# A 16-sample attention and graph-convolution kernel: a new order of work on every engine

## The reference

```
x = x + attention(_gn(x))                  # _gn: groups of 2 channels
    q = softmax(q over 32 channels of a head) * scale;  k = softmax(k over 1024 pixels)
    context = k @ v^T;  out = context^T @ q;  out = w_out @ out + b_out
    out = normalised over the whole sample, * gn_weight + gn_bias
x = x + graph_conv(_gn(x))
    xn  = pixels' 64-vectors scaled to length 1;  sim = xn @ xn^T      # 1024 x 1024 per sample
    val, idx = top_k(sim, 9);  v = val / sum(val)
    out = sum over 9 neighbours of v * (xn @ w1) + b1;  group norm (4 groups), silu
    out = sum over the same neighbours of v * (out @ w2) + b2;  group norm, silu
```

## Time and profile before

| | us |
|---|---|
| median of 3 runs | 694.48 (687.77 to 695.98) |
| the profiled execution | 693.69 |
| its span, first to last instruction | 691.9 |
| TensorE busy, share of the span | 623.0, 90% |
| VectorE | 536.2, 77% |
| GpSimd | 499.6, 72% |
| ScalarE | 449.3, 65% |
| DMA queue of SyncE, share of 16 engines | 38.8% |
| granted TensorE clock, mean | 0.978 |

### The profile page before, as it was taken

One profiled execution on the slowest core, in us unless ns is written; L12 is line 12 of the kernel. 1 busy time (PEld: TensorE's weight loads), 2 busy tenths in 40 slices (PEclk: granted clock), 3 DMA queues, 4 the chain that ended last, 5 costly groups with the idle time before them and its releaser, 6 DMA issues.

```text
span 691.9 us, 12330 instructions
## 1 busy us (share of the span) xinstructions
PE 623.0 (90%) x3821; PEld 312.0 (45%) x3821; DVE 536.2 (77%) x1008; ACT 449.3 (65%) x942; POOL 499.6 (72%) x534
## 2 busy tenths in 40 slices
PE   7787979898999999998999999998989999889984
PEld 5563635344353535353444535353534444333441
DVE  2238788888898989888898889898888988857821
ACT  2236658586786878585867768786858687643321
POOL 0122787868787888888797978888887979786810
PEclk9999999999999999999999999999999999979997
DMA  3002343434354444435353535435343634454311
GB/s 93 0 17 46 71 83 78 91 71 107 83 102 84 100 85 93 92 83 102 76 110 77 108 76 107 85 86 103 83 96 71 108 63 101 82 96 88 62 32 31
DMA packets 148722, 55.76 MB, mean 81 GB/s; under 512 B 138008, under 2 KB 138512, under 8 KB 148656
## 3 DMA queue, kind: packets, MB, share of 16 engines
q1 hardware_dynamic: 148656, 54.97, 38.8%
HBM read 12.87 MB, written 4.32 MB: 25 GB/s over the span
## 4 chain that ended last, share of the span: by engine, by line
PE 31%; POOL 25%; issue 16%; DVE 10%; DMA 9%; ACT 7%; SPq 1%; POOLq 0%; ACTq 0%; DVEq 0%
PE pC L967 17%; POOL adj L389 10%; POOL adj L384 5%; PE pS L923 4%; DMA rbc<-rn_row 4%; DMA rn_row<-rnT 4%; POOL qn L348 3%; ACT adj L527 2%; PE pB L768 2%; POOL res L407 2%; DVE kstat L607 2%; ACT ek L458 2%; PE pA L807 2%; POOL xn L372 2%; DVE top L676 2%
## 5 line engine op out<-in xcount | busy, mean ns | idle before, releaser
L967 PE MATMUL pC<-adj,xt 128*64 128x512 f32 x992 | 233.2, 603 | 3.1 <-POOL adj L395 1.8
L389 POOL TENSOR_TENSOR adj<-maskT,adj 128x128 f32<-128x128 f16 (+3 forms) x127 | 163.6, 1288 | 28.2 <-DMA maskT<-mask 25.3
L676 DVE MAX8 top<-pS 128x8 f32<-128x1024 f32 x128 | 155.6, 1224 | 30.7 <-ACT adj L527 30.5
L694 DVE MATCH_REPLACE8 mask<-top,pS 128x1024 uint16<-128x1024 f32 x128 | 155.3, 1213 | 0.0
L923 PE MATMUL pS<-xn 64*128 64x512 f32 x256 | 145.3, 655 | 6.2 <-issue 5.6
L923 PE MATMUL pS<-xn,xsw 64*128 64x512 f32 x256 | 144.7, 656 | 2.9 <-DVE mask L694 2.9
L527 ACT COPY adj<-pS 128x1024 f32<-128x1024 f32 x128 | 128.3, 1004 | 27.3 <-PE pS L925 27.1
L384 POOL TENSOR_TENSOR adj<-maskT,adj 128x128 f32<-128x128 f16 (+6 forms) x111 | 128.5, 1158 | 0.0
L967 PEld LDWEIGHTS pC<-adj,xt 128*64 128x64 f32 x992 | 63.9, 137 | 103.6 <-issue 96.0
L395 POOL TENSOR_TENSOR adj<-adj,selves 128x128 f32<-128x128 f32 x127 | 58.7, 462 | 8.7
L925 PEld LDWEIGHTS pS<-mark,place 64*128 64x128 f16 x256 | 24.5, 96 | 76.1 <-issue 76.1
(11 more groups left out here) (153 smaller groups left out, 1101.7 us busy)
## 6 DMA issues: line engine op xcount, KB each, us to landing
xs<-x SPq DMA_DIRECT2D x32, 128.0 KB, 2.8
vbc<-v_row SPq DMA_DIRECT2D x32, 128.0 KB, 2.9
rbc<-rn_row SPq DMA_DIRECT2D x30, 128.0 KB, 2.8
xsw<-xn SPq DMA_DIRECT2D x30, 128.0 KB, 2.4
out<-res SPq DMA_DIRECT2D x30, 128.0 KB, 2.4
maskT<-mask SPq DMA_TRANSPOSE x128, 3.1
cst<-packed SPq DMA_DIRECT2D x1, 471.5 KB, 3.9
y1sw<-y SPq DMA_DIRECT2D x2, 128.0 KB, 2.3
```

The lines of the kernel that those rows point to most:

```text
L389: pool.tensor_tensor(above, m[:, r, 0:r + 1, :].bitcast(F16), above, ALU.mult).then_inc(done["upper"], 1)
L676: dve.max(top[b % 2][:, r, 0:TOP], pS[r % 2][:, :]).then_inc(done["tile_top"], 1)
L694: dve.match_replace(out=mask[n % MASKS][:, :], in_to_replace=top[b % 2][:, r, 0:TOP], in_values=pS[r % 2][:, :], imm_value=ONE_BITS).then_ ...
L967: mm = pe.matmul(ps[h * C:(h + 1) * C, 0:H], xt[:, t % NJ, t // NJ, :], adj[b % 2][:, t, h * H:(h + 1) * H], start=(t == 0), stop=(t == NT ...
```

## The change

The single list `BEGINS` becomes three, one each for attention and unit, for the tile stages, and for convolve; `PARTS` says which stage takes which list. All the offsets in `TIMES` are replaced, and so is `WARM`: 318 fillers become 390 (a group for `("q", 1)` is in the table, but no step asks for it). In four places waits of TensorE follow the new order, and one call of `warm` is dropped. No instruction that computes is added or removed.

```diff
-BEGINS = [0, 40.3551, 80.6227, 121.0734, 161.3839, 202.0138, 242.3515, 282.6959, 323.22, 363.5685, 404.1094, 444.49,
...
+PARTS = {"inputs": 0, "attend": 0, "unit": 0, "weights": 1, "itself": 1, "neighbours": 1, "tops": 1, "masks": 1, "marks": 1, "convolve": 2}
+BEGINS = [
...
-    ("start", 0): 36, ("k", 0): 20, ("ekT", 0): 9, ("qT", 0): 8, ("att", 0): 7, ("at_mean", 0): 16, ("in_mean", 1): 6,
-    ("mi_mean", 0): 32, ("k", 1): 9, ("ss", 0): 4, ("att", 1): 6, ("sim1", 0): 2, ("mi_mean", 1): 24, ("k", 2): 9,
-    ("xt1", 1): 24, ("g1_mean", 14): 18, ("sim7", 15): 12, ("g2_mean", 14): 18, ("g1_mean", 15): 12, ("xt2", 15): 21,
-    ("a2_0", 15): 5, ("ky", 0): 20,
+    ("start", 0): 36, ("k", 0): 24, ("ekT", 0): 9, ("qT", 0): 8, ("att", 0): 8, ("at_mean", 0): 19, ("in_mean", 1): 10,
+    ("mi_mean", 0): 39, ("k", 1): 17, ("q", 1): 8, ("att", 1): 9, ("in_mean", 2): 10, ("sim4", 0): 16, ("mi_mean", 1): 10,
+    ("k", 2): 13, ("xt1", 1): 18, ("sim0", 1): 16, ("att", 2): 9, ("g1_mean", 14): 2, ("sim7", 15): 13, ("xt2", 14): 7,
+    ("g2_mean", 14): 11, ("g1_mean", 15): 12, ("xt2", 15): 29, ("a2_0", 15): 4, ("g2_mean", 15): 21, ("ky", 0): 20,
...
-                    live += [(BEGINS[b] + at, steps) for at in TIMES[engine][stage.__name__]]
+                    live += [(BEGINS[PARTS[stage.__name__]][b] + at, steps) for at in TIMES[engine][stage.__name__]]
...
                 if b < 1:
                     pe.wait_ge(*of("in_veps", b))
+                elif b < 2:
+                    pe.wait_ge(*of("ss_read", b - 1, 2))
                 else:
                     pe.wait_ge(*of("mi_veps", b - 1))
...
-                warm("ss", b)
                 pe.wait_ge(*of("sq_ready", b))
-                if b < 15:
+                if b < 1:
+                    pe.wait_ge(*of("mi_veps", b))
+                elif b < 15:
                     pe.wait_ge(*of("yT_copied", b + 1))
...
                 pe.wait_ge(*of("rn_ready", b))
-                if b < 2:
+                if b < 1:
+                    pe.wait_ge(*of("yT_copied", b + 1))
+                elif b < 2:
                     pe.wait_ge(*of("ss_read", b, 2))
```

More of the change, by code:

```diff
@@ L29 @@
 PACKED = CONST_PARTS + WEIGHT_PARTS + [(name, 1) for name in VECTORS]
-BEGINS = [0, 40.3551, 80.6227, 121.0734, 161.3839, 202.0138, 242.3515, 282.6959, 323.22, 363.5685, 404.1094, 444.49,
-          485.0099, 525.4191, 565.7534, 605.859]
+PARTS = {"inputs": 0, "attend": 0, "unit": 0, "weights": 1, "itself": 1, "neighbours": 1, "tops": 1, "masks": 1, "marks": 1, "convolve": 2}
+BEGINS = [
+    [0, 43.7679, 84.6436, 125.8457, 167.2382, 207.6013, 248.8792, 289.8169, 330.7721, 372.2689, 413.5082, 454.2157, 495.8963,
+     536.5253, 577.4959, 618.5594],
+    [0, 40.7602, 81.636, 122.8463, 163.4119, 204.6215, 245.3367, 286.5808, 327.994, 369.0126, 409.9847, 451.4971, 492.2687,
+     533.3503, 573.6684, 613.2583],
+    [0, 40.9091, 81.6341, 122.584, 163.4381, 204.3951, 245.6569, 286.9489, 328.1214, 369.3658, 410.7502, 451.3767, 492.5799,
+     532.9203, 574.8846, 614.585],
+]
 TIMES = {
@@ L37 @@
         "attend": [0],
-        "unit": [122.814, 124.0739, 139.8554],
-        "neighbours": [144.5435, 146.5376, 153.5254, 159.4181, 159.4182, 168.0831, 180.5052, 181.0079],
-        "convolve": [199.2326, 199.2327, 265.073],
+        "unit": [89.7538, 96.4524, 103.3671],
+        "neighbours": [120.9276, 121.1054, 133.105, 133.1051, 133.1052, 143.4386, 152.7499, 160.4412],
+        "convolve": [169.202, 170.4109, 233.8618],
     },
     "gpsimd": {
-        "attend": [60.859, 84.8058],
-        "unit": [99.5701, 99.5702, 104.0019, 106.8089, 112.4974],
@@ L45 @@
[L45 to L48, removed]
+        "attend": [58.9225, 84.1612],
+        "unit": [90.8105, 96.6084, 105.8733, 110.5569, 119.5039],
+        "weights": [138.195, 140.4417, 144.0865, 144.0866, 146.2015, 149.0325, 150.4153, 151.0194, 151.0195, 151.0196,
+            155.3908, 157.5535, 157.6905, 157.6906, 158.8454, 168.3563, 168.3564, 168.3565, 171.6202, 171.8558, 171.8559,
+            174.0678, 174.9659],
@@ L49 @@
+        "convolve": [197.0726, 216.224, 247.7607],
     },
     "scalar": {
[L51 to L55, removed]
+        "attend": [54.954, 68.1936, 73.202, 79.3721, 79.4966, 82.3873, 85.7675, 90.3689, 96.448, 99.9077],
@@ L56 @@
+        "unit": [102.8428, 103.1491, 108.1034, 112.4021, 112.5656, 119.7064, 119.7065],
+        "itself": [140.6896, 140.6897, 141.0712, 141.7673, 160.9092, 161.1155, 170.0966, 176.4743],
+        "neighbours": [137.2313, 137.2314, 137.2315, 145.7707, 150.3167, 156.0239, 166.0749, 168.6294, 174.597],
+        "convolve": [206.1627, 207.4391, 209.1732, 213.9436, 226.7754, 228.2281, 250.906],
     },
     "vector": {
-        "attend": [41.1532, 58.5568, 59.4218, 66.1132, 71.553, 75.9608, 79.508, 79.5081, 80.2525],
@@ L59 @@
[L59 to L62, removed]
+        "attend": [56.6882, 66.1966, 69.6355, 74.5737, 82.6445, 85.657, 88.3368, 88.5975, 91.6332],
@@ L63 @@
+        "unit": [101.2271, 104.0211, 104.0212, 108.6247, 111.448, 114.2833, 120.2284, 124.081],
+        "tops": [142.6241, 142.6242, 147.386, 149.6306, 153.4303, 166.0678, 172.9647, 176.2671, 177.6285],
+        "masks": [142.6243, 144.5297, 147.8408, 155.9545, 161.6818, 169.4198, 175.7906, 177.6284],
+        "convolve": [186.1089, 200.2018, 201.9682, 207.9946, 209.9176, 225.2501, 225.2502, 228.4968, 232.0305],
     },
     "tensor": {
-        "attend": [62.5654, 65.5492, 67.2037, 68.7244, 73.8243, 73.8244, 77.4149, 81.5063, 83.5364],
@@ L66 @@
[L66 to L69, removed]
+        "attend": [67.4254, 73.7624, 76.3568, 80.0414, 84.1194, 84.1195, 90.1868, 95.9204, 98.7833],
@@ L70 @@
+        "unit": [107.0568, 112.9669, 119.8097, 123.5018],
+        "neighbours": [139.2941, 139.2942, 139.6546, 144.569, 150.0711, 153.8006, 162.8519, 166.7426, 172.1272],
+        "convolve": [187.4328, 191.8625, 193.1332, 193.1333, 196.2842, 197.449, 197.4491, 198.6026, 198.9424, 207.0373,
+            212.2597, 218.8724, 219.4407, 219.4408, 219.4409, 220.1953, 223.7745, 223.7746, 223.7747, 230.8169],
     },
```

## The result

| | before | changed |
|---|---|---|
| median, us | 693.64 (687.77 to 695.98, 4 runs) | 702.12 (698.52 to 707.8, 4 runs) |
| the profiled execution | 693.69 | 707.8 |
| its span | 691.9 | 706.0 |
| mean granted TensorE clock | 0.978 | 0.967 |

The ratio is 1.014, with a 95% interval of 1.0092 to 1.0188. The forecast was 693.7, with a range up to 702.0. The four executions of the changed kernel fall into two pairs: 698.5 us twice at a mean granted clock of 0.983 and 0.984, and 705.7 and 707.8 us at 0.972 and 0.967. The profile is of the last, so what it shows of the clock is more than the typical execution loses.

The account below looks back on a forecast made before the run. A loop over several engines was taken to close each period, with TensorE idling 1 to 3 us. Periods +1.2, fill -1.0, drain -1.0 sum to -0.8, so 693.7 us against a median of 694.48; range 684 to 702.

Parts of the forecast that it names:

- Path B: Period's end through `qn`, its transposes, second half of products, VectorE's second mask, fourth similarity; 0.16 us shorter than `res` and diagonals.
- the two moves: In the periods: `res` ahead of `qn` on GpSimd, a later sample's load no longer directly ahead of `rn_row`; together +1.2 us.
- the row: 4 KB write `rn_row` on SyncE's queue: without the load ahead, 1.2 to 1.6 us; gain 0.5 us per period.
- the three periods in which GpSimd idled behind `xn`: GpSimd idle 1.19 us until tile 5's transposed mask landed; `res` fills the hole free, -0.65 us each, -2.0.
- rival 2: Periods: the row gets no faster and `res` costs in full, 8.7 us; total 701.2 us, chance 0.18.
- rival 3: Periods: `res` costs nothing anywhere, -9.2 us; total 683.3 us, or 679 if the drain keeps its clock; chance 0.18.
- rival 4: Tile 2's transpose arrives late behind load, `v_row` and `vbc`, up to 1.5 us per period; total 712 us, chance 0.08.
- the other fillers: 72 added fillers, 8.6 us, outside sample 1's first similarity: stand where TensorE waits anyway; overruns of 0.2 to 0.8 left in range.
- the term of -1.5 in the fill: 16 fillers ahead of sample 1's first similarity take 1.9 us, just TensorE's idle time, and hold the clock: -1.5 us.
- The queries came 3.0 us later, not 1.6: Fill: sample 1's queries wait for the keys' turn and copy, +1.6 us, of which +0.5 remains by the next keys.
- The 0.4 for the earlier squares: Fill: sample 0's squares come earlier, which takes 0.4 us off the delay of sample 1's queries.
- The drain, -1.0: Drain: ScalarE copies sample 15's tile 5 earlier, -0.8 us; shorter wait ahead of `xt2`, -0.2 us.

Follow-up runs that it names:

- the kernel that ran twice: Changed kernel without the 7 fillers ahead of `xt2` of sample 14, `res` and `out` at their old places: 683.73 us (ratio 0.985), then 683.3 (0.9861).

## Why the prediction was wrong

**The bound and the two moves: right.** Path B had next to nothing to spare, the row fell from about 2.0 to 1.19, `res` costs 1.1 per period alone, and both together gave +1.1 for a forecast of +1.2. The single terms can't be checked one by one in one pair of traces, for the profiled twelve periods went to +4.3. None was to take 39 us, and one takes 40.0 and one 39.4: in the first the row takes 3.37, in the second the read back follows it 2.69 us later (464.16 to 466.85), where 1.2 is usual, and ahead of `xn` GpSimd idles 2.66 and 2.08 us. Executions scatter by that much: the kernel before with seven fillers in the drain, its periods unchanged, took 458.8 for them against 454.5. One reading was loose: of the three periods in which GpSimd idled behind `xn`, the profile names the transposed mask in two (1.19 and 1.01 us) and ScalarE's `selves` in the third (1.04); the price is the same.

**Rivals 2, 3 and 4: not what happened.** The row got faster (against 2), `res` was not free (against 3), and tile 2's transpose never held GpSimd up (against 4). One sign that the prediction named for rival 4 did show: GpSimd waits longer for the transposed mask of tile 3, 1.4 to 1.5 us in all but the first period, where it was 0.8 to 1.0:

```profile
379.98 1.16 POOL L389 TENSOR_TENSOR adj<-maskT,adj 128x512 f32<-128x512 f16 x1 [0.85 <-DMA maskT<-mask]
```
```profile
384.42 1.16 POOL L396 TENSOR_TENSOR adj<-maskT,adj 128x512 f32<-128x512 f16 x1 [1.47 <-DMA maskT<-mask]
```

It delays nothing. Tile 3 starts 3.5 us after TensorE's keys in the kernel before (379.98 - 376.51) and 3.4 in the changed one (384.42 - 380.98); only GpSimd's work ahead of it ends 0.6 us earlier. That the time is near rival 2's is chance: its 8.7 us belong to the periods, while the missing ones lie in the drain and the fill.

**The fillers: the step that failed.** It is the sentence that "the other fillers (+72 in all, 8.6 us) stand where TensorE waits anyway", with the term of -1.5 in the fill, which rests on the same thought. Both price the matmuls by their number and leave out where the waits stand that go with them. The kernel was in view ahead of the prediction, with the three choices of a bank in `warm` and the place of `warm` in `similarity`.

- In the drain the seven ahead of `xt2` of sample 14 bring a wait for a mask that nothing else on TensorE waited for there. TensorE stands 2.97 us for it, and with the clock behind it the profile shows 6.5 us lost, for a forecast of nothing. Without the wait the ratio is 1.0047, with it 1.014: 6.4 us.
- In the fill the sixteen ahead of sample 1's first similarity were to run in the idle time of 1.90 us and hold the clock, for -1.5. They stand behind the wait (1.86 us, then the fillers at 92.75), and cost 1.6 us on average. In this execution they ran at the lower clock themselves, 3.49 us for the 1.9 booked. Nor did the clock need them each time: with the load alone moved it was 1.00 from 86 to 98 without them.

**The rest of the fill.** The queries came 3.0 us later, not 1.6. The 0.4 for the earlier squares was not gained, since the matmuls that spread `rn` began at 46.51 against 46.57 in the earlier trace rows; the profile names ScalarE's copy `yT` as what they now waited for. The turn ran at the lower clock (1.82 us, where 1.0 was booked), and the queries then waited 1.10 for the copy: 50.12 + 1.82 + 1.10 = 53.04. Where the clock held, 1.1 us was the whole price, so this term had the right sign and about the right size.

**The drain, -1.0: right in sign.** Where the wait is away, it is 691.7 - 565.8 = 125.9 from sample 15's keys to the end, 1.0 below the 126.9 of before. The other profiles scatter, and together show more: with `res` at its old place 127.0 in the old order and 124.9 in the changed one (2 and 4 profiles), with `res` moved 129.4 and 125.9 (2 and 3).

**The sum.** By the ratios: both moves +0.24%; the fill and drain order with them +0.53%; the mask wait up to +1.4%, which is 9.7 us (the medians differ by 8.5). About 6.4 of them are the step that was missed in the drain. The other miss is that fill and drain were booked at -2.0 and gave about +2 (0.53% against 0.24%, which the intervals leave open by some 3 us either way); the fillers ahead of the first similarity make some 3 us of it, 1.6 in place of -1.5.

## What to carry to other kernels

Price an inserted instruction by the waits that come with it, the helper's as well, and ask of the semaphore when it was last raised in the trace of before and when it will be in the new order. A filler fills an idle time only if it is issued ahead of the wait that makes it; behind that wait it is work added. Where two moves share a change, time them apart: one here made the kernel 1.5% faster and the other 2.0% slower, and together they looked like nothing.

## What the runs showed of the hardware that was not expected

- A 4 KB write from SBUF to DRAM took 1.18 to 1.22 us in each row that the chains of waits show of the kernel with the load moved and of that with both moves, where no load was issued just ahead of it in SyncE's queue, and 1.7 to 2.4 behind two loads of 128 KB (kernel before and that with `res` moved; one took 3.54). The Trainium skill, "DMA: Bandwidth & Descriptors", section "Anatomy of one DMA — SWDGE (gpsimd) path", has about 2.0 us as the fixed part, told of DMAs that GpSimd issues; on SyncE's queue the 1.19 are less.
- The load ahead is not the only thing that slows the row. In the changed order no load stands there, and most rows take 1.2, but in seven of the eight profiles of this order one to three rows take 2.5 to 3.6 us. In the two kernels above none of 30 did. What holds these up is open.
- The clock is not the same in each execution of one order. Of the kernel that ran twice the profile has it at 0.57 from 46 to 50 us in one execution and at 1.00 in the other, and the eight transposes of the keys took 1.85 us in the one and 1.09 in the other.
- An idle time of 1.71 us in the drain left the clock at the upper level, and one of 2.97 us was followed by the lower one for some 10 us (0.50 from 656 to 666). In that execution the delay was 3.1 us of the loss and the clock 3.4.
